# Moving one add of the softplus from VectorE to ScalarE in a Mamba and mixture-of-experts kernel, with new instruction lists

## What is computed

```python
u = silu(conv4(in_proj_w @ ctx) + conv_b)
dt_lo, Bm, Cm = split(x_proj_w @ u)
delta = softplus(dt_proj_w @ dt_lo + dt_proj_b)
state = state * exp(delta * A) + (delta * u) * B_t       # for each of 256 tokens
y = (state . C_t + D * u) * silu(layernorm(x))
x = x + tanh(g_xattn) * y
h = layernorm(x); scores = sigmoid(h @ gate_w.T)         # top 2 of 8, normalised, times 2.5
x = x + tanh(g_ffn) * (shared(h) + sum of the picked experts(h))
```

## Time and profile before

| | us |
|---|---|
| median of 3 runs (250.77 to 251.74) | 251.2 |
| the profiled execution | 251.53 |
| its span in the trace | 249.7 |
| around the span | 1.8 |

### The profile page before, as it was taken

One profiled execution on the slowest core, in us unless ns is written; L12 is line 12 of the kernel. 1 busy time (PEld: TensorE's weight loads), 2 busy tenths in 40 slices (PEclk: granted clock), 3 DMA queues, 4 the chain that ended last, 5 costly groups with the idle time before them and its releaser, 6 DMA issues.

```text
span 249.7 us, 3695 instructions
## 1 busy us (share of the span) xinstructions
PE 215.2 (86%) x878; PEld 149.9 (60%) x878; DVE 205.3 (82%) x494; ACT 164.8 (66%) x497; POOL 184.2 (74%) x228
## 2 busy tenths in 40 slices
PE   4973994387889987679998899899999999999995
PEld 1942863263446854446665576577677677677774
DVE  0726999998999989998999999999899898663330
ACT  2377999997698877659569997759556472341320
POOL 0655838999999999999999999899996876400000
PEclk9995699679999999999999999999999999999999
DMA  6408699969760202020743020302000000000000
GB/s 204 175 4 245 197 302 416 341 220 342 246 243 20 84 21 83 1 85 13 248 169 105 1 85 1 106 0 85 21 3 21 1 4 1 21 0 0 3 21 21
DMA packets 26965, 25.97 MB, mean 104 GB/s; under 512 B 1080, under 2 KB 25920, under 8 KB 26304
## 3 DMA queue, kind: packets, MB, share of 16 engines
q1 hardware_dynamic: 26512, 25.06, 30.5%
q10 hardware_dynamic: 432, 0.68, 0.9%
HBM read 24.56 MB, written 1.18 MB: 103 GB/s over the span
## 4 chain that ended last, share of the span: by engine, by line
PE 46%; POOL 17%; DMA 11%; issue 10%; SPq 8%; DVE 5%; ACT 2%; ACTq 0%; DVEq 0%; POOLq 0%
PE psU L662 21%; PE psD L537 15%; POOL acc L1065 9%; DMA brows<-xdbl 6%; POOL dbu L1019 5%; PE psM L640 3%; SPq L502 3%; SPq L492 3%; DMA bb<-brows 3%; DVE psH L911 2%; PE psU L658 2%; DMA win<-in_w_in 2%; PE psM L565 2%; PE psD L565 1%; PE psH L544 1%
## 5 line engine op out<-in xcount | busy, mean ns | idle before, releaser
L662 PE MATMUL psU<-wup,hnT 128*128 128x352 f32 x288 | 95.7, 466 | 7.5 <-DVE hcat L841 4.4
L1019 POOL TENSOR_TENSOR dbu<-du,bb 128x512 f32<-128x512 f32 x64 | 80.7, 1276 | 9.5 <-DVE du L455 6.0
L688 ACT ACTIVATE psA<-delta,aneg 128x127 f32<-128x127 f32 x256 | 77.9, 357 | 2.8 <-DVE psH L911 2.8
L911 DVE TENSOR_TENSOR_SCAN psH<-psA,dbu 128x512 f32<-128x512 f32 x64 | 76.8, 1220 | 1.6 <-issue 0.9
L662 PEld LDWEIGHTS psU<-wup,hnT 128*128 128x128 f32 x288 | 51.4, 190 | 36.5 <-DVE hcat L841 10.6
L1065 POOL TENSOR_TENSOR acc<-acc,prod 128x512 f32<-128x512 f32 x42 | 53.4, 1271 | 4.2 <-DVE prod L921 2.9
L805 ACT ACTIVATE tg<-psU 128x176 f32<-128x176 f32 x80 | 24.9, 315 | 45.5 <-PE psU L662 45.2
L537 PE MATMUL psD<-wdn,hT 128*128 128x256 f32 x224 | 52.1, 380 | 0.1
L537 PEld LDWEIGHTS psD<-wdn,hT 128*128 128x128 f32 x224 | 41.8, 190 | 7.8 <-DVE x_sb L954 0.8
L921 DVE TENSOR_TENSOR prod<-psH,cc 128x512 f32<-128x512 f32 x64 | 42.3, 680 | 1.1 <-POOL acc L1065 0.8
L993 DVE SCALAR_TENSOR_TENSOR ag<-tg,psU 128x176 f32<-128x176 f32 x80 | 25.7, 330 | 17.6 <-ACT tg L805 17.0
(11 more groups left out here) (107 smaller groups left out, 212.1 us busy)
## 6 DMA issues: line engine op xcount, KB each, us to landing
cc<-brows SPq DMA_DIRECT2D x16, 512.0 KB, 4.4
bb<-brows SPq DMA_DIRECT2D x3, 2048.0 KB, 7.1
wup<-in_w_up SPq DMA_DIRECT2D x1, 1760.0 KB, 11.6
wdn<-in_w_down SPq DMA_DIRECT2D x1, 1664.0 KB, 15.3
wup<-in_w_up SPq DMA_DIRECT2D x1, 1408.0 KB, 7.8
x_sb<-in_x SPq DMA_DIRECT2D x4, 256.0 KB, 5.3
bb<-brows SPq DMA_DIRECT2D x1, 1024.0 KB, 7.1
out<-outb SPq DMA_DIRECT2D x8, 128.0 KB, 1.7
```

Source lines behind the costliest of these rows:

```text
L662: last = pe.matmul(dst, hnT[:, b % 2, k, lh * P:(lh + 1) * P], wup[:, j - 1, k, :], start=(k == 0), stop=(k == KT - 1))
L688: last = act.activation(dst[:, j, h, 1:], delta[:, b % 2, h, l0 + 1:l1], ACT.Exp, scale=aneg[:, h * DS + s0 + j:h * DS + s0 + j + 1])
L911: dve.tensor_tensor_scan(psH[:, i % 2], psA[:, i % DA_RING], dbu[:, i % DBU_RING], 0.0, ALU.mult, ALU.add).then_inc(s_scan, 1)
L1019: pool.tensor_tensor(tile(dbu[:, m % DBU_RING], m), du[:, b % 2, :, l0:l1].unsqueeze(1).broadcast_to(shape), bb[:, b % 2, s0:s0 + ns, l0:l ...
```

## The change

`log_1`, which writes 1 + e into `dy`, moves from VectorE (a `tensor_scalar` with add) to ScalarE (an ACTIVATE of the function Copy with bias 1). It reads the same PSUM tile and waits for the same things. All five `log_1` tasks leave VectorE's list and enter ScalarE's, each between `soft_exp` and `soft_log` of its piece. The lists of TensorE, ScalarE, VectorE and GpSimd are written anew; SyncE's is unchanged. No other instruction is added or taken away.

The code:

```diff
@@ ScalarE
+                elif task == "log_1":
+                    b, l0, l1 = piece(i)
+                    act.wait_ge(s_exp, i + 1)
+                    if i >= LH:
+                        act.wait_ge(s_del, i)
+                    act.activation(dy[:, :, l0:l1], split(soft(i)), ACT.Copy, bias=1.0).then_inc(s_dy, 1)
@@ VectorE
-                elif task == "log_1":
-                    dve.wait_ge(s_exp, i + 1)
-                    if i >= LH:
-                        dve.wait_ge(s_del, i)
-                    b, l0, l1 = piece(i)
-                    dve.tensor_scalar(dy[:, :, l0:l1], split(soft(i)), 1.0, None,
-                                      ALU.add).then_inc(s_dy, 1)
```

The lists, cut to the stretches that matter here:

```diff
     "TensorE": """
-        project:0 project:1 xproj:0 dt:0 xproj:1 dt:1 project:2 prod:0 prod:1 prod:2 prod:3 xproj:2 dt:2 prod:4
-        prod:5 prod:6 prod:7 y_sum:0 to_tokens:0 project:3 to_features:0 up:0 up:1 up:2 up:3 xproj:3 up:4 up:5
...
-        to_tokens:4 up:31 down:8 down:9 turn:10 up:32 up:33 turn:11 down:10 up:34 up:35 turn:12 down:11 up:36
...
-        down:23 up:64 up:65 to_tokens:7 up:66 turn:24 up:67 up:68 turn:25 to_features:7 up:69 up:70 turn:26
...
+        project:0 project:1 xproj:0 dt:0 xproj:1 dt:1 project:2 prod:0 prod:1 prod:2 xproj:2 prod:3 dt:2 prod:4
+        prod:5 prod:6 prod:7 y_sum:0 to_tokens:0 project:3 to_features:0 up:0 up:1 up:2 up:3 up:4 xproj:3 up:5
...
+        up:23 down:6 down:7 turn:8 up:24 up:25 up:26 up:27 turn:9 up:28 dt:4 to_features:3 up:29 to_tokens:4
+        up:30 up:31 down:8 down:9 up:32 turn:10 up:33 turn:11 down:10 down:11 up:34 up:35 turn:12 up:36 turn:13
...
+        up:64 to_tokens:7 up:65 up:66 turn:24 up:67 up:68 turn:25 to_features:7 up:69 up:70 down:24 up:71
     "ScalarE": """
-        load:0 project_out:0 z_norm:0 project_out:1 tanh_u:0 tanh_u:1 xproj_out:0 dt_out:0 soft_exp:0
-        xproj_out:1 soft_log:0 dt_out:1 soft_exp:1 first:0 soft_log:1 scan:0 scan:1 scan:2 skip:0 z_gate:0
-        project_out:2 tanh_u:2 scan:3 scan:4 decay:0 xproj_out:2 scan:5 scan:6 dt_out:2 soft_exp:2 scan:7 scan:8
-        soft_log:2 scan:9 scan:10 scan:11 z_norm:1 scan:12 scan:13 z_gate:1 norm:0 scan:14 to_features_out:0
+        load:0 project_out:0 z_norm:0 project_out:1 tanh_u:0 tanh_u:1 skip:0 xproj_out:0 dt_out:0 xproj_out:1
+        soft_exp:0 log_1:0 soft_log:0 dt_out:1 soft_exp:1 log_1:1 soft_log:1 first:0 scan:0 scan:1 scan:2
+        z_gate:0 decay:0 project_out:2 tanh_u:2 scan:3 scan:4 xproj_out:2 scan:5 scan:6 dt_out:2 scan:7 scan:8
+        z_norm:1 soft_exp:2 log_1:2 scan:9 scan:10 soft_log:2 z_gate:1 scan:11 scan:12 scan:13 norm:0 scan:14
     "VectorE": """
-        load:0 z_stats:0 z_stats:1 z_stats:2 z_stats:3 silu_u:0 silu_u:1 log_1:0 log_2:0 delta0:0 delta1:0
-        delta2:0 log_1:1 log_2:1 scan:0 scan:1 prod:0 keep_ends:0 keep_ends:1 prod:1 scan:2 delta0:1 scan:3
-        delta1:1 prod:2 prod:3 keep_ends:2 keep_ends:3 silu_u:2 z_gate:0 scan:4 scan:5 prod:4 keep_ends:4
-        keep_ends:5 prod:5 delta2:1 scan:6 scan:7 prod:6 prod:7 keep_ends:6 keep_ends:7 log_1:2 scan:8 scan:9
-        gate_y:0 prod:8 prod:9 scan:10 scan:11 prod:10 log_2:2 scan:12 residual:0 stats:0 prod:11 variance:0
-        scan:13 prod:12 prod:13 scan:14 scan:15 prod:14 gate:0 route:0 mul:0 gate:1 prod:15 mul:1 silu_u:3
-        scan:16 gate:2 gate:3 keep_ends:16 mul:2 mul:3 scan:17 prod:16 prod:17 gate:4 scan:18 gate:5
...
-        gate:29 prod:42 mul:29 scan:44 residual:4 log_1:4 gate:30 gate:31 route:3 log_2:4 mul:30 mul:31 prod:43
...
+        load:0 z_stats:0 z_stats:1 z_stats:2 z_stats:3 silu_u:0 silu_u:1 log_2:0 delta0:0 delta1:0 delta2:0
+        log_2:1 delta0:1 scan:0 scan:1 keep_ends:0 prod:0 prod:1 scan:2 keep_ends:1 delta1:1 scan:3 z_gate:0
+        prod:2 silu_u:2 keep_ends:2 keep_ends:3 prod:3 scan:4 scan:5 prod:4 prod:5 keep_ends:4 keep_ends:5
+        delta2:1 scan:6 scan:7 keep_ends:6 prod:6 keep_ends:7 prod:7 scan:8 scan:9 prod:8 prod:9 gate_y:0
+        scan:10 scan:11 residual:0 stats:0 variance:0 log_2:2 prod:10 prod:11 scan:12 scan:13 prod:12 prod:13
+        scan:14 prod:14 scan:15 gate:0 route:0 mul:0 gate:1 mul:1 silu_u:3 prod:15 gate:2 mul:2 scan:16 gate:3
+        scan:17 keep_ends:16 gate:4 mul:3 prod:16 mul:4 prod:17 scan:18 gate:5 keep_ends:17 mul:5 scan:19
...
+        finish:1 scan:41 gate:28 mul:27 mul:28 scan:42 prod:41 prod:42 gate:29 residual:4 mul:29 scan:43 scan:44
+        route:3 gate:30 gate:31 mul:30 mul:31 log_2:4 stats:4 prod:43 prod:44 scan:45 scan:46 gate:32 gate:33
     "GpSimd": """
-        scan:13 fix:13 prod:10 scan:14 variance:0 fix:14 delta0:2 fix:15 prod:11 delta1:2 prod:12 delta2:2
-        scan:15 prod:13 scan:16 prod:14 scan:17 prod:15 scan:18 scan:19 prod:17 scan:20 scan:21 prod:18 scan:22
...
-        fix:40 prod:37 fix:41 variance:3 prod:38 carry:5 scan:42 fold:4 fix:42 fix:43 scan:43 prod:39 fix:44
-        fold2:4 gate_y:4 scan:44 prod:41 scan:45 scan:46 fix:45 fix:46 fix:47 delta0:4 prod:42 delta1:4 prod:43
...
+        scan:13 variance:0 prod:10 fix:13 fix:14 prod:11 scan:14 delta0:2 fix:15 delta1:2 prod:12 delta2:2
+        prod:13 scan:15 scan:16 prod:14 scan:17 scan:18 prod:15 prod:17 scan:19 scan:20 prod:18 scan:21 scan:22
...
+        fix:40 scan:40 prod:37 fix:41 scan:41 prod:38 fold:4 fix:42 prod:39 carry:5 fold2:4 scan:42 gate_y:4
+        scan:43 fix:43 fix:44 scan:44 prod:41 scan:45 scan:46 prod:42 fix:45 fix:46 fix:47 delta0:4 prod:43
```

More of the change, by code:

```diff
@@ L185 @@
-        keep_ends:17 keep_ends:18 mul:4 mul:5 prod:18 scan:19 scan:20 gate_y:1 prod:19 keep_ends:19 keep_ends:20
-        gate:6 scan:21 mul:6 keep_ends:21 residual:1 gate:7 prod:20 mul:7 log_1:3 gate:8 prod:21 scan:22 scan:23
-        log_2:3 mul:8 stats:1 keep_ends:22 keep_ends:23 variance:1 gate:9 mul:9 prod:22 prod:23 z_gate:1 scan:24
-        scan:25 prod:24 finish:0 prod:25 scan:26 prod:26 scan:27 gate:10 route:1 mul:10 gate:11 scan:28 mul:11
-        gate_y:2 prod:27 prod:28 gate:12 gate:13 mul:12 mul:13 scan:29 silu_u:4 scan:30 gate:14 gate:15 mul:14
@@ new lines @@
+        scan:14 prod:14 scan:15 gate:0 route:0 mul:0 gate:1 mul:1 silu_u:3 prod:15 gate:2 mul:2 scan:16 gate:3
+        scan:17 keep_ends:16 gate:4 mul:3 prod:16 mul:4 prod:17 scan:18 gate:5 keep_ends:17 mul:5 scan:19
+        prod:18 keep_ends:18 gate_y:1 scan:20 gate:6 gate:7 keep_ends:19 mul:6 mul:7 prod:19 prod:20 scan:21
+        z_gate:1 residual:1 keep_ends:20 keep_ends:21 stats:1 scan:22 log_2:3 keep_ends:22 variance:1 gate:8
+        gate:9 mul:8 mul:9 prod:21 prod:22 scan:23 scan:24 keep_ends:23 prod:23 prod:24 scan:25 finish:0 prod:25
@@ new lines @@
+        scan:26 scan:27 prod:26 prod:27 gate:10 route:1 mul:10 gate:11 gate_y:2 mul:11 scan:28 prod:28 gate:12
+        silu_u:4 gate:13 mul:12 mul:13 scan:29 scan:30 gate:14 residual:2 mul:14 stats:2 gate:15 mul:15 prod:29
+        prod:30 scan:31 gate:16 gate:17 mul:16 mul:17 variance:2 scan:32 prod:31 prod:32 scan:33 gate:18 gate:19
+        mul:18 mul:19 keep_ends:32 keep_ends:33 gate_y:3 prod:33 scan:34 residual:3 prod:34 scan:35 gate:20
+        gate:21 keep_ends:34 keep_ends:35 stats:3 scan:36 route:2 mul:20 mul:21 variance:3 prod:35 prod:36
@@ new lines @@
+        prod:47 finish:2 gate:37 mul:37 gate:38 mul:38 scan:49 gate:39 prod:48 mul:39 gate:40 route:4 mul:40
+        gate:41 keep_ends:48 keep_ends:49 residual:5 mul:41 stats:5 prod:49 variance:5 scan:50 gate:42 gate:43
+        mul:42 mul:43 scan:51 keep_ends:50 keep_ends:51 prod:50 prod:51 scan:52 scan:53 prod:52 gate:44 gate:45
+        keep_ends:52 keep_ends:53 mul:44 mul:45 scan:54 finish:3 gate:46 keep_ends:54 mul:46 gate:47 mul:47
+        prod:53 prod:54 gate:48 mul:48 scan:55 z_gate:3 gate:49 gate:50 mul:49 route:5 keep_ends:55 mul:50
@@ new lines @@
+        scan:56 prod:55 gate:51 gate:52 mul:51 mul:52 scan:57 prod:56 scan:58 gate:53 gate:54 mul:53 prod:57
+        prod:58 mul:54 finish:4 scan:59 gate:55 residual:6 mul:55 stats:6 variance:6 gate:56 mul:56 scan:60
+        gate:57 mul:57 prod:59 prod:60 gate:58 gate:59 mul:58 mul:59 scan:61 scan:62 prod:61 prod:62 gate:60
+        gate:61 route:6 mul:60 mul:61 scan:63 prod:63 gate:62 mul:62 finish:5 gate:63 mul:63 gate:64 mul:64
+        residual:7 stats:7 gate:65 mul:65 variance:7 gate:66 mul:66 gate:67 mul:67 gate:68 mul:68 gate:69 mul:69
@@ L211 @@
+        route:7 gate:70 mul:70 gate:71 mul:71 gate:72 mul:72 gate:73 mul:73 gate:74 mul:74 gate:75 mul:75
+        gate:76 gate:77 mul:76 mul:77 gate:78 mul:78 finish:6 gate:79 mul:79 finish:7
     """,
@@ L223 @@
[L223 to L227 removed]
+        scan:6 scan:7 fix:8 scan:8 scan:9 fix:9 carry:1 fix:10 scan:10 scan:11 fix:11 fix:12 prod:9 scan:12
@@ L228 @@
+        scan:55 scan:56 fix:56 fix:57 scan:57 prod:53 prod:54 fix:58 fold:6 prod:55 fold2:6 scan:58 scan:59
+        carry:7 fix:59 fix:60 scan:60 gate_y:6 prod:57 scan:61 variance:6 scan:62 fix:61 prod:58 fix:62 fix:63
+        prod:59 prod:60 prod:61 prod:62 fold:7 prod:63 fold2:7 gate_y:7 variance:7
     """,
```

96 lines of the change are left out of this document (37 added, 59 removed).

## The result

| | before | after |
|---|---|---|
| median, us | 251.37 (4 runs, 250.77 to 251.74) | 254.58 (4 runs, 253.59 to 255.22) |
| span of the profiled execution, us | 249.7 | 251.8 |
| mean granted clock of TensorE, share of full | 0.966 | 0.959 |
| busy: TensorE, VectorE, GpSimd, ScalarE, us | 215.2, 205.3, 184.2, 164.8 | 215.4, 206.1, 184.8, 166.5 |

The ratio is 1.0127, 95% interval 1.0081 to 1.0172. The forecast was 250.1 us, the range ended at 252.6. In this document a median is taken over all executions of a kernel, while a ratio and its interval leave out those over 1.5% above the fastest of their kernel.

What follows compares the result with a forecast made beforehand. VectorE and GpSimd bound 60 to 140 us, then TensorE. Start-up +0.5, middle -1.8 and -0.4, anchor change 0.1 give -1.6; end +0.5 gives -1.1 us: 250.4 for the profiled execution, 250.1 median, range 248.0 to 252.6.

Steps and rivals of the forecast that it cites:

- the middle: After step 17 to `mul:30`: VectorE saves 1.8 us by `log_1:3`, `log_1:4`, `log_2:4`, and 0.4 of its wait for `acc`.
- late decays at step 12: Rival: ScalarE late with step 12's decays delays `scan:12` and both full engines; at 3 us late, 252.6 us; chance 0.17.
- The sign of being wrong: VectorE's idle time between 60 and 145 us grows by what the copies freed, or TensorE waits anew after 145 us.
- the anchor: TensorE's start of `turn:10` (old, 145.13 us) or `up:32` (new), with the same tasks left; forecast 1.6 us earlier.
- end: `to_tokens:7` stands one `up` earlier in TensorE's list, so TensorE waits for its tile: +0.5 us.
- The copy: `log_1` on ScalarE takes 0.58 us (large) and 0.37 us (small); no table load added, nine in both lists.
- The start-up: Steps 0 to 17: `scan:12` waits 0.4 us, `scan:17` at 63.9 instead of 63.65 us, `mul:3` not yet done; +0.5 us.
- GpSimd's pace: Rival: GpSimd, full from 60 to 140 us, sets the pace; VectorE's freed slots become waits; 251.0 us, chance 0.22.

Runs made afterwards that it cites:

- GpSimd held back: Changed kernel with one added wait: GpSimd does not start the `dbu` of step 24 before `z_gate:1` is done; 250.38 us, ratio 0.995 to the kernel before.
- operand in PSUM: Changed kernel with `z_gate:1` reading its first operand from PSUM (`psH`) in place of the tanh in SBUF; 249.29 us, ratio 0.9919 to the kernel before.
- two buffers: Changed kernel with a second buffer for `sz`, `z_gate:1` moved behind `prod:11` and ahead of `scan:12`; 249.76 us, ratio 0.9904 to the kernel before.

## Why the prediction was wrong

**The failed step** is in the part on the middle: "VectorE's two lists hold the same tasks, but for the five `log_1` and for `log_2:4`". It is true, and I drew from it that their durations are the same too. `z_gate:1` had moved by two scans, from 82.6 to 75.3 us, and I priced that at nothing without naming it. It took 3.80 in place of 1.50 us. The three microseconds over its own 0.68 held up `residual:1` and with it TensorE, TensorE's delay and its low clock held up `hidden:2` and the decays behind it, and VectorE waited for these by another 1.94 us. The row that warned was there: 1.50 us, where the other three of its kind took some 0.68. The rivals did not have it either; a loss was to come from late decays at step 12, where VectorE waited 0.63 us for a forecast 0.4. Late decays did come, at step 24, but as a consequence. The sign of being wrong that I had named, VectorE's idle time, could hardly show it: from 60 to 140 us that is 3.5 us where it was 2.8, since an instruction that is shut out counts as busy.

Six profiled executions, cut at the start of `scan:17` and at the anchor, show where the time went (us):

| kernel | `scan:17` | anchor | between |
|---|---|---|---|
| before (anchor `turn:10`) | 63.65 | 145.13 | 81.5 |
| changed (anchor `up:32`, here and below) | 63.34 | 147.06 | 83.7 |
| changed, once more | 64.12 | 148.15 | 84.0 |
| GpSimd held back | 65.34 | 144.84 | 79.5 |
| operand in PSUM | 62.37 | 141.95 | 79.6 |
| two buffers | 65.65 | 145.20 | 79.6 |

The block costs 4.1 to 4.5 us between the two points; by the medians of the three kernels without it, it is 4.2 to 5.3. Without it the stretch is 1.9 us shorter than before.

**The rest, point by point.** The anchor was well chosen. From the anchor to the end of the span the kernel before has 249.7 - 145.13 = 104.6 us, and the changed one 251.8 - 147.06 = 104.7:

```profile
147.06 1.45 PE L661 MATMUL psU<-wup,hnT 128*128 128x352 f32 x4
```

With the operand in PSUM it is 246.6 - 141.95 = 104.65 us. So the *end*, for which I had added 0.5 us, cost 0.2 at most, and no idle time of TensorE stands before `to_tokens:7`. The anchor itself came 1.9 us late where -1.6 was forecast.

*The copy* was right: 0.595 and 0.38 us, nine table loads. Groups of ScalarE by shape:

```profile
L817 ACT COPY hT<-psM 128x512 f32<-128x512 f32 x24 | 14.0, 582 | 7.6 <-PE psM L639 7.0
...
L743 ACT ACTIVATE dy<-psM 128x512 f32<-128x512 f32 x3 | 1.8, 595 | 0.1
```

*The start-up* cannot be judged from one execution. Forecast: `scan:8` 40.7, `scan:12` 49.9 with a wait of 0.4, first `gate:0` 57.45, `scan:17` 63.9. VectorE's timeline, which answers to the earlier trace rows:

```profile
39.96 2.33 DVE L909 TENSOR_TENSOR_SCAN psH<-psA,dbu 128x512 f32<-128x512 f32 x2
...
49.55 2.49 DVE L909 TENSOR_TENSOR_SCAN psH<-psA,dbu 128x512 f32<-128x512 f32 x2 [0.63 <-ACT psA L687]
...
57.02 0.32 DVE L991 SCALAR_TENSOR_TENSOR ag<-tg,psU 128x176 f32<-128x176 f32 x1
...
63.34 1.22 DVE L909 TENSOR_TENSOR_SCAN psH<-psA,dbu 128x512 f32<-128x512 f32 x1
```

Here `scan:17` is 0.3 us earlier than before, not 0.25 later. But in five traces whose lists are the same up to there it lies between 62.37 and 65.34 us, and already the first scan between 22.37 and 25.29. Against that neither my +0.25 nor the measured -0.3 means anything. One forecast of this part did fail: `prod:13` in front of it does not cover GpSimd's wait before the `dbu` of step 16. That wait is 0.34 us here, and 0.47 and 0.72 in the kernels with the operand in PSUM and with two buffers, where it was 0.45:

```profile
59.90 1.27 POOL L1017 TENSOR_TENSOR dbu<-du,bb 128x512 f32<-128x512 f32 x1 [0.34 <-issue]
```

*The middle without the block.* From `scan:17` to the anchor the forecast amounts to -1.6 - 0.25, some -1.9 us, and that is what the three kernels without the block show. In part this is luck. The kernel before had itself lost 0.8 us to the 1.50 us row, which the forecast did not count; VectorE's wait of 0.80 us for `acc` is gone whole and not by half, and a new wait of 0.49 us for a `gate` has come. By the medians the kernel whose GpSimd waits is 1.0 us below the kernel before where 1.1 was forecast, the one with the operand in PSUM 2.1 below, and the one with two buffers 1.9. The last two are nearly twice the forecast; the 0.5 us that I had put on the end accounts for part of that, the start-up stays open. *GpSimd's pace* was near the truth in one way: nothing but GpSimd's unbroken row of instructions made the block so long. But its rival was priced as waits for `dbu` and `acc`, on semaphores, and this was none.
